# First attention stage of a two-layer graph network: tokens normalised tile by tile, target one-hot vectors partly on ScalarE

## The reference, cut to what matters

```
xn = _layernorm(x, axis=-1)
q, k, v = split(xn @ w_map.T); k = layernorm_per_head(k); v = layernorm_per_head(v)
attn = einsum('bhnd,bhne->bhde', k, v) / n
mix  = einsum('bhnd,bhde->bhne', q, attn) @ w_out.T + b_out
x = x + gnn(xn, edge_index) + mix
```

## Time and profile before

| | us |
|---|---|
| median of 3 runs (2012.62 to 2015.86) | 2013.35 |
| the profiled execution | 2008.69 |
| its span, first to last instruction | 2006.8 |
| PE, DVE, ACT busy in the span | 1863.9, 1308.7, 907.6 |

### The profile page before, as it was taken

The page is one execution under the profiler, slowest core; times in us unless marked ns, Lnnn a source line. Parts: engine busy times, 40 slices in busy tenths (PEclk is TensorE's granted clock), DMA queues, the critical chain, the costliest instruction groups (busy, mean ns, idle before and its releaser), DMA issues.

```text
span 2006.8 us, 30851 instructions
## 1 busy us (share of the span) xinstructions
PE 1863.9 (93%) x12197; PEld 1770.5 (88%) x12198; DVE 1308.7 (65%) x2466; ACT 907.6 (45%) x1503; POOL 154.4 (8%) x129
## 2 busy tenths in 40 slices
PE   5997998899999999778779999999999999999998
PEld 4885788899889999778668999999999999999998
DVE  6997765645345657888874664346565666676886
ACT  2321221424233635666434223236555565666776
POOL 0000000004000013322120000000101001001010
PEclk8997998999999999888889999999999999999999
DMA  3110001101122112110122132245656667676895
GB/s 115 48 48 1 24 25 71 63 24 49 48 71 87 72 38 75 40 38 17 72 74 87 48 103 72 71 163 198 210 198 218 218 215 241 222 259 237 284 326 200
DMA packets 36796, 234.30 MB, mean 117 GB/s; under 512 B 5916, under 2 KB 7318, under 8 KB 14632
## 3 DMA queue, kind: packets, MB, share of 16 engines
q1 hardware_dynamic: 31318, 217.41, 30.5%
q0 software_dynamic: 2656, 8.99, 2.0%
q10 hardware_dynamic: 2674, 5.87, 0.8%
HBM read 221.91 MB, written 10.35 MB: 116 GB/s over the span
## 4 chain that ended last, share of the span: by engine, by line
PE 75%; DVE 12%; issue 7%; ACT 4%; DMA 1%; POOL 0%; ACTq 0%; DVEq 0%; SPq 0%; POOLq 0%
PE bank L341 16%; PE bank L342 15%; PE bank L343 15%; PE bank L2671 8%; PE bank L665 4%; PE bank L2683 3%; PE bank L2672 3%; DVE weight_lo L314 2%; PE bank L2687 2%; PE bank L2684 2%; PE bank L2675 2%; ACT weight_hi L304 1%; PE bank L2686 1%; DVE mix_kv L888 1%; PE bank L2674 1%
## 5 line engine op out<-in xcount | busy, mean ns | idle before, releaser
L314 DVE TENSOR_TENSOR weight_lo<-weight_raw,weight_hi 128x2304 fp32r<-128x2304 f32 (+1 forms) x155 | 393.3, 2541 | 40.5 <-ACT weight_hi L304 40.4
L304 ACT ACTIVATE weight_hi<-weight_raw 128x2304 fp32r<-128x2304 f32 (+1 forms) x155 | 323.2, 2087 | 71.7 <-DMA weight_raw<-in_ffn_w 51.2
L341 PE MATMUL bank<-xT_hi,weight_hi 128*128 128x320 f32 (+1 forms) x576 | 182.0, 316 | 1.4 <-issue 1.4
L342 PE MATMUL bank<-xT_lo,weight_hi 128*128 128x320 f32 (+1 forms) x576 | 177.2, 308 | 0.0
L343 PE MATMUL bank<-xT_hi,weight_lo 128*128 128x320 f32 (+1 forms) x576 | 176.9, 307 | 0.0
L3045 DVE TENSOR_TENSOR hidden_tmp<-hidden_tmp,bank 128x160 f32<-128x160 f32 (+5 forms) x192 | 65.6, 342 | 159.4 <-ACT hidden_tmp L2831 159.4
L341 PE MATMUL bank<-weight_hi,xT_hi 128*128 128x384 f32 (+1 forms) x480 | 161.5, 336 | 8.0 <-DVE xT_lo L362 4.5
L342 PE MATMUL bank<-weight_lo,xT_hi 128*128 128x384 f32 (+1 forms) x480 | 157.3, 328 | 0.0
L343 PE MATMUL bank<-weight_hi,xT_lo 128*128 128x384 f32 (+1 forms) x480 | 157.3, 328 | 0.0
L665 PE MATMUL bank<-one_hot_dst,one_hot_src 125*128 125x313 f16 x800 | 122.6, 304 | 15.2 <-ACT packed_counts L679 7.9
L2831 ACT ACTIVATE hidden_tmp<-bank,ffn_b_by_load 128x160 f32<-128x160 f32 (+5 forms) x192 | 73.4, 402 | 119.5 <-PE bank L2675 117.4
(11 more groups left out here) (498 smaller groups left out, 5062.6 us busy)
## 6 DMA issues: line engine op xcount, KB each, us to landing
weight_raw<-in_ffn_w SPq DMA_DIRECT2D x111, 1152.0 KB, 5.2
weight_raw_fifth<-in_ffn_w SPq DMA_DIRECT2D x25, 1152.0 KB, 5.4
weight_raw<-in_shared_w SPq DMA_DIRECT2D x16, 1152.0 KB, 5.1
weight_raw<-in_mix_kv SPq DMA_DIRECT2D x8, 1152.0 KB, 5.1
weight_raw<-in_gat_w SPq DMA_DIRECT2D x8, 768.0 KB, 4.4
weight_raw<-in_mix_q SPq DMA_DIRECT2D x4, 1152.0 KB, 5.0
weight_raw<-in_mix_out SPq DMA_DIRECT2D x4, 1152.0 KB
weight_raw<-in_gnn_w SPq DMA_DIRECT2D x4, 1152.0 KB, 5.1
```

The costliest lines, as they stand in the source:

```text
L304: act.activation(upper_, whole_, ACT.Copy).then_inc(*w_hi.one())
L314: dve.tensor_tensor(lower_, whole_, upper_.bitcast(F32), ALU.subtract).then_inc(*w_lo.one())
L341: pe.matmul(dst, a[0], b[0], start=first, stop=False)
L342: pe.matmul(dst, a[0], b[1], start=False, stop=False)
```

## The change

`first_sync` loads each tile of `x` by a DMA of its own, the first two ahead of the first weight chunk and of the edges, the others behind them. `tile_norm` replaces `layer_norm` for the first stage (its other uses stay). The first 21 columns (`BOTH`) are made as before. From the 22nd on DVE makes the sources only; ACT makes the targets from a squared distance, Square((t - iota) / 4), and Relu(p - 16 p s) with p = 1 or 4096. Their two operands are prepared once by DVE.

```diff
@@ first_sync
-        sp.dma_start(x[:, 0:TT - 1, :], ins["x"][0:(TT - 1) * P, :].rearrange("(t p) d -> p t d", p=P)).then_inc(*x_in.dma())
+        def tile(t):
+            sp.dma_start(x[:, t, :], ins["x"][t * P:(t + 1) * P, :]).then_inc(*x_in[t].dma())
+        tile(0)
+        tile(1)
+        weights_load(1)
         for n, name in enumerate(("src", "dst")):
...
+        tile(2)
+        tile(3)
+        sp.wait_ge(blank.semaphore, 1)
...
         weights_load(DEPTH - 1)
@@ counting_attention
+        BOTH = sum(FIRST) + AHEAD
+        columns["target"] = BOTH
...
+            own_step(dve.tensor_scalar(edge[:, 3, :], edge[:, 2, :], -16.0, None, ALU.mult))
+            own_step(dve.tensor_scalar(edge[:, 1, BOTH:EC], edge[:, 1, BOTH:EC], 0.25, None, ALU.mult))
...
-                dve.tensor_scalar(hot_dst[:, j % HOT, :], iota_h[0:EP, 0:320], edge[:, 1, j:j + 1], edge[:, 2, j:j + 1],
-                                  ALU.is_equal, ALU.mult).then_inc(*hot.one())
+                if j < BOTH:
+                    dve.tensor_scalar(hot_dst[:, j % HOT, :], iota_h[0:EP, 0:320], edge[:, 1, j:j + 1], edge[:, 2, j:j + 1],
+                                      ALU.is_equal, ALU.mult).then_inc(*hot.one())
...
-                pe.wait_ge(*hot.at(2 * (j + 1)))
+                if j < BOTH:
+                    pe.wait_ge(*hot.at(2 * (j + 1)))
+                else:
+                    pe.wait_ge(*hot.at(BOTH + j + 1))
+                    pe.wait_ge(*hot_target.at(j - BOTH + 1))
...
+        def targets_scalar(n):
+            for j in range(columns["target"], min(columns["target"] + n, EC)):
+                act.wait_ge(*hot_used.at(j - HOT + 1))
+                act.activation(hot_dst[:, j % HOT, :], iota_h[0:EP, 0:320], ACT.Square, bias=edge[:, 1, j:j + 1], scale=-0.25).then_inc(*squared.one())
+                act.wait_ge(*squared.now())
+                act.activation(hot_dst[:, j % HOT, :], hot_dst[:, j % HOT, :], ACT.Relu, bias=edge[:, 2, j:j + 1],
+                               scale=edge[:, 3, j:j + 1]).then_inc(*hot_target.one())
+            columns["target"] = min(columns["target"] + n, EC)
+        def columns_scalar(n):
+            for _ in range(n):
+                targets_scalar(1)
+                edges_scalar(1)
@@ tensor(): keys_or_values, per tile, and the start
+                    if n == 0:
+                        if 2 <= t + 1 < TT:
+                            norm.turn_tensor(t + 1)
+                        pe.wait_ge(*norm.ready[t])
...
-            pe.wait_ge(*xT_ready)
+            pe.wait_ge(constants.semaphore, 2)
+            norm.turn_tensor(0)
+            norm.turn_tensor(1)
@@ first_vector_steps (new, ahead of vector())
+            moments_of(0)
+            norm.scale_vector(0)
+            moments_of(1)
+            norm.scale_vector(1)
+            norm.lower_vector(0)
+            norm.lower_vector(1)
+            dve.memset(zeros[:, :, :], 0.0).then_inc(*pads_blank.one())
+            edges_ready()
@@ scalar(): every edges_scalar after n = 0 becomes columns_scalar; the start
+            norm.root_scalar(0)
+            norm.root_scalar(1)
+            norm.upper_scalar(0)
+            norm.upper_scalar(1)
+            weight_hi(0)
+            norm.root_scalar(2)
+            norm.upper_scalar(2)
+            act.wait_ge(*edges_read)
+            act.wait_ge(*constants.now())
             for t in range(TT):
                 copied(0, t)
                 edges_scalar(FIRST[t])
+                if 3 <= t + 3 < TT:
+                    norm.root_scalar(t + 3)
+                    norm.upper_scalar(t + 3)
+                if t == 2:
+                    weight_hi(1)
@@ vector()
-            edges_vector(sum(FIRST) + AHEAD)
+            edges_vector(2)
+            weight_lo(0)
+            ahead = 2
+            for t in range(2, TT):
+                moments_of(t)
+                edges_vector(2)
+                norm.scale_vector(t)
+                edges_vector(FIRST[t - 2] - 2)
+                norm.lower_vector(t)
+                ahead += FIRST[t - 2]
+            edges_vector(2)
+            weight_lo(1)
+            edges_vector(sum(FIRST) + AHEAD - ahead - 2)
```

More of the change, by code:

```diff
@@ L384, in program @@
     constants, ones_made = sig("constants_made"), sig("ones_made")
-    x_in, edges_in_ = sig("x_landed"), sig("edges_landed")
+    x_in, edges_in_ = [sig("x_landed0"), sig("x_landed1")] + [sig("x_landed")] * (TT - 2), sig("edges_landed")
     blank = sig("blank_made")
@@ L407, in first_sync @@
     def first_sync():
-        sp.dma_start(x[:, 0:TT - 1, :], ins["x"][0:(TT - 1) * P, :].rearrange("(t p) d -> p t d", p=P)).then_inc(*x_in.dma())
-        sp.wait_ge(blank.semaphore, 1)
-        for a0, n in parts_of_16(LAST):
-            sp.dma_start(x[a0:a0 + n, TT - 1, :], ins["x"][(TT - 1) * P + a0:(TT - 1) * P + a0 + n, :]).then_inc(*x_in.dma())
+        def tile(t):
[3 more added lines that the diff above has]
+        weights_load(1)
         for n, name in enumerate(("src", "dst")):
@@ L414, in first_sync @@
                 sp.dma_start(edges_i[a0:a0 + rows, n, :], ins[name][a0:a0 + rows, :]).then_inc(*edges_in_.dma())
+        tile(2)
+        tile(3)
+        sp.wait_ge(blank.semaphore, 1)
+        for a0, n in parts_of_16(LAST):
+            sp.dma_start(x[a0:a0 + n, TT - 1, :], ins["x"][(TT - 1) * P + a0:(TT - 1) * P + a0 + n, :]).then_inc(*x_in[TT - 1].dma())
         weights_load(DEPTH - 1)
@@ L424, in program, with layer_norm @@
     first_scalar()
-    def layer_norm(xn, *x_ready, scalar_meanwhile=None, vector_meanwhile=None):
+    def layer_norm(xn, *x_ready):
         var, std, normed, turned, xT_hi, xT_lo = sigs("ln_variance", "ln_deviation", "ln_normed", "xT_turned", "xT_hi", "xT_lo")
@@ L577, in counting_attention @@
             "pads_blank", "pads_hi", "pads_lo")
-        gains_in = sig("gains_landed")
+        gains_in, squared, hot_target = sig("gains_landed"), sig("edge_acted"), sig("edge_made")
         scope = ExitStack()
@@ L608, in counting_attention @@
         edge_banks = psum[3:8]
-        columns = {"tensor": 0, "scalar": 0, "vector": 0}
+        columns = {"tensor": 0, "scalar": 0, "vector": 0, "target": 0}
         FIRST = (4, 4, 3, 3, 3)
@@ L757, in tensor, with moments_of, first_vector_steps @@
                     project(n // 3, PROJECTION if n == 2 else 0)
+        def moments_of(t):
+            dve.wait_ge(*x_in[t].now())
+            norm.stats_vector(t)
+        def first_vector_steps():
+            moments_of(0)
[6 more added lines that the diff above has]
+            edges_ready()
+            return dve_own.now()
         def scalar():
@@ L790, in following @@
                     query(i // 2, i % 2)
-                edges_scalar(STEP[i])
+                columns_scalar(STEP[i])
             def query(n, s):
@@ L810, in queries @@
                     query(n, s)
-                    edges_scalar(beside)
+                    columns_scalar(beside)
             def attend(n):
@@ L819, in attend @@
                     upper(at(outT, ALL, n % 3, slice(a0, a0 + wide)), o_banks[i][:, 0:wide]).then_inc(*o_hi.one())
-                    edges_scalar(pair_columns(n))
+                    columns_scalar(pair_columns(n))
+            norm.root_scalar(0)
[7 more added lines that the diff above has]
+            act.wait_ge(*constants.now())
             for t in range(TT):
@@ L828, in scalar @@
             upper(at(qp, ALL, ALL, pads), zeros[:, 0:2, :]).then_inc(*pads_hi.one())
-            edges_scalar(sum(HEADS_LEFT))
+            columns_scalar(sum(HEADS_LEFT))
             act.wait_ge(*heads_kept.at(12))
@@ L844, in scalar @@
                 if n == 2:
-                    edges_scalar(2 * TT * PROJECTION)
+                    columns_scalar(2 * TT * PROJECTION)
             weight_read[c0 + 6] = out_full.at(2 * TT)
@@ L941, in project @@
                             unpack(CHUNKS - 1, step)
-            dve.memset(zeros[:, :, :], 0.0).then_inc(*pads_blank.one())
-            edges_vector(sum(FIRST) + AHEAD)
+            edges_vector(2)
[11 more added lines that the diff above has]
+            edges_vector(sum(FIRST) + AHEAD - ahead - 2)
             for n in range(4):
@@ L967, in vector @@
             weights_lo(c0 + 7)
[L969 to L980, removed]
         ring.banks, ring.until, ring.k = psum[0:3], ring.until[0:3], 0
+        norm = tile_norm(xn)
+        xT_ready = norm.ready[-1]
         tensor()
+        edges_read = first_vector_steps()
         scalar()
```

4 lines of the change are left out of this document (removed).

## The result

The changed kernel takes 2018.62 us (median of ten runs), the kernel before beside it 2014.82 (ten runs): a ratio of 1.0028, 95% interval 1.0017 to 1.0039. By the ratio it is slower by 0.28%, 5.6 us; the two medians are 3.8 us apart. I had forecast 2.9 us less and "same". The value lies at the upper edge of my range. The forecast of the direction was wrong, and the rival that describes what happened is B.

The account below looks back on a forecast made before the run. The stage was taken as bound by PE at both ends and DVE in the middle. Terms -6.6 - 3.6 + 2.8 + 4.5 summed to -2.9 us: 2005.8 profiled, 2010.4 as a median; range 1998 to 2019.

Parts of the forecast that it names:

- rival B: Pairs of heads: ACT is the bound at 1.09 us a column, kernel slower by 6.3 us, 2019.7; chance 0.17.
- Term 1: Kernel start: PE begins 12.3 us earlier, tile turns give back 5.7; -6.6 us, bounds -8.5 and -1.5.
- Rival D: Kernel start: first tile's DMA shares engines and lands near 9.6 us; +2.2 us, 2015.6; chance 0.05.
- Rival C: Start: PE's clock halves behind each of three tile turns, 4.2 us; sum +1.3, 2014.7; chance 0.06.
- Term 2: Up to the second `per_head`: DVE relieved of 67 target columns; -3.6 us, bounds 0 and -18.
- Term 3: Pairs of heads 0 to 2: ACT's queue, 44.3 us against PE's 42.3, delays PE; +2.8 us, bounds 0 and +9.
- The ten output products: Behind the pairs of heads: PE needs 2.93 us for each, ACT 1.8, so the targets cost nothing.
- Term 4: Last weight: its product starts 3.1 us late, slowed matmuls add 1.4; +4.5 us, bounds +1 and +6.
- the Relu as releaser: Middle of n = 3 and pairs of heads: PE released by the targets' Relu, not by L637.
- ACT's full time: Between 198 and 240 us: ACT busy near 100%.
- `per_head(1)` at 179: Second join in the first stage: PE reaches it near 179 us.
- attention at 193: First stage, behind the second join: attention begins near 193 us.

Follow-up runs that it names:

- e1_tiles_only: The changed kernel with all targets made by DVE again, so the new start alone; 2004.22 us, ratio 0.9957 to the kernel before.
- e8_again: The changed kernel unaltered, profiled a second time; 2018.35 us in one run.
- e2_targets_only: The kernel before with its old start, plus ACT making target columns 21 to 159; 2026.33 us, ratio 1.0066 to the kernel before.
- e4_imm_scale: The changed kernel with Relu's scale a constant in place of one number a row; 2018.18 us, ratio 1.0025 to the kernel before.
- e7_weight_first: The changed kernel with ACT making the last weight's upper half ahead of the last early pair's columns; 2015.24 us, ratio 1.0012 to the kernel before.
- e5_until92: The changed kernel with ACT making only target columns 21 to 91, DVE the rest; 2005.25 us, ratio 0.9954 to the kernel before.
- e12: The target columns of `e10` joined to the tile turns of `e11`; 1994.94 us, ratio 0.9913 to the kernel before.
- e11: `e1_tiles_only` with the next tile turned right behind a product, not right ahead of the next; 2000.93 us, ratio 0.9946 to the kernel before.
- e9: The changed kernel with ACT making only target columns 21 to 50, with constant scale; 1999.66 us, ratio 0.9950 to the kernel before.
- e10: `e9` with target columns 55 to 65 and 70 to 80 also made by ACT; 2001.14 us, ratio 0.9954 to the kernel before.

## Why the prediction was wrong

**Term 1, the start: right.** First key product at 17.31 us (17.4 forecast), the first tile's statistics at 4.12, a wait of 1.11 us for ACT's copy before the products of tiles 1 to 3, and the product of n = 1 at 51.80 for 58.28: -6.5 for -6.6. With the new start alone, in `e1_tiles_only`, it is -6.8. (My parts add to 17.2 and not to 17.4, which changes nothing.) Rival D is out by the 4.12 us. Rival C is out as well: behind each turn, a stretch of 1.9 us with transposes and standing only, the first matmul lasts 0.41 us and the next start 0.17 apart. These distances decide it; the granted clock of 1.00 over the first 60 us would not, since it is also shown for the first product, whose matmuls start 0.32 us apart as in the old kernel. The rule of the Trainium skill (TensorE: Matmul & The Clock Gate, Part 4: PE-mode transpose) that transposes do not count as busy had no price here.

**Term 2, DVE's relief: -0.2 for -3.6.** From the first product of n = 1 to the wait in n = 3 the old kernel needs 67.0 us (58.28 to 125.32), the new one 69.9 (51.80 to 121.70): +2.9 for the +1.1 that I had counted. I had the place wrong, too. The block of n = 3, where 3.60 us of waiting for DVE became 2.46 for ACT and 0.31, came out even. The loss is one block earlier, where I had counted nothing. First ACT's copy of the counts stands behind two target columns, 2.28 us: PE waits 0.77 for it and takes the four columns in 3.24 us for 2.57, 1.6 us in all. Then ACT's next columns stand behind that copy, an upper half and five squares, which costs 1.3:

```profile
81.31 1.70 ACT L709 ACTIVATE packed_counts<-bank 128x313 int32<-128x313 f32 x5
82.87 1.83 ACT L359 ACTIVATE mix_kv_hi<-mix_kv 128x1920 fp32r<-128x1920 f32 x1
84.56 2.20 ACT L830 ACTIVATE kv_square<-mix_kv 128x384 f32<-128x384 f32 x5
87.00 0.49 ACT L818 ACTIVATE mix_kv<-bank 128x384 f32<-128x384 f32 x1 [0.23 <-DVE mix_kv_lo L362]
87.39 0.55 ACT L688 ACTIVATE one_hot_dst<-iota_half,edges 125x320 f16<-125x320 f16 x1
```

and PE takes these three columns one at a time, each as it comes (88.77 to 91.05 above). From there to the join the new kernel gains 3.0 us (60.6 for 63.7; I had counted 4.7), since the last block of columns again waits 2.36 for ACT. Together they give -0.2, and with the start -6.7 at the join.

**Term 3, the pairs of heads: +9.8 and +7.0 for +2.8, its upper bound +9.** This is the step that failed, and with it the direction. I priced a column at 0.50 + 0.41 = 0.91 us, from squares and copies of the earlier trace rows that have no bias and no scale from memory, and a square's pitch of 0.47. The square starts the Relu after 0.58 and the Relu the next square after 0.56. The dependence I had priced about right: 0.03 between the two instructions of a column, and an overlap of some 0.06, measured 0.09, with the next. What failed are the durations, 0.55 and 0.65 us for 0.47, which fits their operands from memory (0.09 shown for the scale, some 0.08 read for each bias). In my own sum for ACT's queue, 36 columns at 0.23 more are 8.3 us: 52.6 us of work against PE's 42.3, and the pairs took 50.7 to 53.5. The clean size of this term is +7.0, as in `e8_again` and `e2_targets_only`; the other 2.8 of the first profile go with two falls of its clock, 0.74 over the first 6.5 us of the pairs and 0.76 from 206 to 213 us, where `e8_again` has 1.00.

That is rival B in place and nearly in price, 1.09 us a column and +6.5 for the pairs; I gave it 0.17. (By its own price the sum is zero at 0.97 us a column, not at 1.0.) That its 2019.7 us is 1.1 from the measured median is in part luck: it meant a change of +6.3, stood on an old median of 2013.35 and not 2014.82, and the medians are 3.8 apart. Its reason was not the right one either. It let the two instructions not overlap with anything, at 0.52 each; they do overlap with the next column, but last longer.

**The ten output products: +1.5 for 0.** "Free, but without slack for a second such job" left out that a backlog of ACT from the pairs arrives there. In `e4_imm_scale`, with 1.05 us a column, it is +0.2.

**Term 4, the last weight: +4.3 for +3.1,** 12 columns at 0.23 more being 2.8, part of which the lead covered. The clock's 1.4 behind it came to 2.3 and 1.7: PE needs 17.1 us (16.5 in `e8_again`) to the wait for x, before 14.8.

The measured sum up to the wait for x, by join, join to attention, pairs, ten, weight, and what is behind it: -6.7 - 3.9 + 9.8 + 1.5 + 4.3 + 2.3 = +7.3 (+7.4 by the unrounded times) in the first profile (319.06 for 311.63), -5.9 + 0.5 + 7.0 + 1.5 + 4.3 + 1.7 = +9.1 (+9.2) in `e8_again` (320.79). The first profile gained 4.4 us on `e8_again` from the join to attention and gave back 2.8 in the pairs, as `e7_weight_first` did (193.30, then 53.3). `e5_until92` gives back 1.7 with no target made by ACT in its pairs, so that much is the clock; whether the rest is too, or an ACT that is ready no earlier, isn't shown. From the graph convolution's first product to the end the two profiles of the changed kernel take 1694.9 and 1687.5 us, the old one 1687.0, all with the same code. That spread is the execution's, and no part of the change.

**Of the signs I had named,** the first product, the statistics, the three short waits, the Relu as releaser and the long wait for the weight (4.52 us) came, and a column costs over 1.0 us, by which I had called the forecast wrong. ACT's full time came in part: 36.80 of the 42 us from 198 to 240, 29.17 of the 30 behind them. `per_head(1)` at 179 did not come (182.34), and attention at 193 came in one profile of two.

What stays open is why the granted clock differs between executions of one kernel at the same place. And `e4_imm_scale` has a shorter stage than `e8_again` by 5.1 us in the profile but the same median as the changed kernel; one profile each does not settle how much of the 0.09 us reaches the end.

## What to carry to other kernels

Price an instruction by a row with the same kinds of operands, not by one of the same shape alone; here 0.23 us a column, on an engine that was to be full, turned a small gain into a loss. Shifting work pays only in the stages where the receiving engine has room and no long wait ahead of the moved piece: 139 targets on ACT cost 12.7 us, 52 of them in the right places gained 6.0 (`e12` against `e11`). In `e9` and `e10` against `e1` such a gain shows at the join, not in the time. A change made of two parts deserves its two halves measured, since a good one (-9.4 us) hid behind a bad one (+12.7).

## What the runs showed of the hardware

- On ScalarE, an activation of 125x320 fp16 lasts 0.562 us with a constant scale and 0.654 with a scale from memory, the bias from memory in both: 0.09 us for one operand.
- In the old kernel an activation of 128x320 fp32 from a bank lasts 0.519 us with a bias from memory and 0.437 as a plain copy.
- A second activation on the result of the first, with a semaphore between, starts 0.58 us after a 0.547 us one: the hand-over costs 0.03, and the rest is the first one's full duration. The activation behind a 0.654 us one on which it doesn't depend starts after 0.56: an overlap of 0.09.
- The granted clock can fall to half behind a short wait, in one execution and not in the next. In the profile after, PE waits 0.74 us, works again at 743.18, and from 744 us on the clock is 0.50 for 9 us, with PE busy all the time. `e8_again` has the same wait before 748.18 us and the kernel before has it before 739.14, and both keep 1.00 (in the old kernel from 740 to 749 us). First after, then `e8_again`:

```profile
743.18 0.33 PE L341 MATMUL bank<-mix_att_hi,mix_q_hi 128*128 128x130 f32 x1 [0.74 <-DVE mix_q_lo L362]
```

```profile
744.00:753.00 9.00, 9.00 (x45) 9.00 (x45) 5.77 (x12) 0.00 (x0) 0.00 (x0) 0.50 0.02 8
```

```profile
749.00:758.00 9.00, 9.00 (x81) 9.00 (x81) 5.91 (x13) 1.42 (x4) 2.96 (x3) 1.00 0.14 32
```
